# Pooling pass of a four-layer graph network: the sum of gathered rows and turned features made by TensorE in PSUM instead of by VectorE

## The reference, cut to what matters

```python
m = node_feats[src] + edge_feats
mx = jax.ops.segment_max(m, dst, num_segments=n)
ex = jnp.exp(m - mx[dst])
denom = jax.ops.segment_sum(ex, dst, num_segments=n)
a = ex / denom[dst]
agg = jax.ops.segment_sum(m * a, dst, num_segments=n)
h = jax.nn.relu(agg @ mlp_w.T + mlp_b)
return h * scale + node_feats
```

## Time and profile before

| | |
|---|---|
| median of three runs | 4112.33 us |
| lowest and highest | 4110.33 and 4114.03 us |
| the profiled execution, its time | 4113.25 us |
| its span in the trace | 4111.4 us |
| first gather of the pooling pass starts at | 3531.25 us |
| last gather of the pooling pass starts at | 4026.06 us |
| last addition of the pass (line 1356) starts at | 4051.14 us |
| share of the span busy: PE, DVE, ACT, POOL | 57%, 53%, 44%, 64% |

### The profile page before, as it was taken

One profiled execution on the slowest core, in us unless ns is written; L12 is line 12 of the kernel. 1 busy time (PEld: TensorE's weight loads), 2 busy tenths in 40 slices (PEclk: granted clock), 3 DMA queues, 4 the chain that ended last, 5 costly groups with the idle time before them and its releaser, 6 DMA issues.

```text
span 4111.4 us, 44915 instructions
## 1 busy us (share of the span) xinstructions
PE 2340.2 (57%) x10010; PEld 1838.4 (45%) x10010; DVE 2173.5 (53%) x5063; ACT 1822.6 (44%) x4227; POOL 2646.8 (64%) x2793
## 2 busy tenths in 40 slices
PE   6777775344442445444555565655655555467765
PEld 4665653343442434342333353434544344356654
DVE  5888873455564555555222223333434444666667
ACT  2887864343432434335434344343254432344543
POOL 4777712777753777744777727777467776477771
PEclk9999997555555555555555578778855555688887
DMA  6555522343422334323555533333267877455551
GB/s 190 151 161 154 161 59 48 78 86 80 84 60 55 81 78 84 77 49 100 156 160 157 159 87 105 105 105 105 62 191 202 217 212 195 124 155 155 158 155 38
DMA packets 589252, 497.67 MB, mean 121 GB/s; under 512 B 73835, under 2 KB 530592, under 8 KB 588656
## 3 DMA queue, kind: packets, MB, share of 16 engines
q0 software_dynamic: 101696, 235.14, 22.8%
q1 hardware_dynamic: 484630, 254.57, 22.3%
q10 hardware_dynamic: 2684, 5.18, 0.4%
HBM read 426.04 MB, written 68.57 MB: 120 GB/s over the span
## 4 chain that ended last, share of the span: by engine, by line
POOL 50%; issue 19%; PE 12%; DVE 12%; DMA 4%; DVEq 1%; ACT 1%; POOLq 0%; SPq 0%; ACTq 0%
POOL big L595 24%; POOL big L608 18%; POOL y_and_h L622 9%; PE ps L741 5%; DVE y_and_h L1384 3%; DMA big<-table_sage,src_block 2%; DVE ps L1376 2%; DVE big L1356 2%; PE ps L664 2%; PE ps L891 1%; PE ps L678 1%; PE ps L888 1%; DVEq L416 1%; DMA big<-table_gat,src_idx 1%; DVEq L1376 1%
## 5 line engine op out<-in xcount | busy, mean ns | idle before, releaser
L595 POOL DMA_INDIRECT big<-table_sage,src_block x1173 | 1109.9, 946 | 559.9 <-issue 346.3
L608 POOL DMA_INDIRECT big<-table_gat,src_idx x832 | 787.6, 947 | 484.7 <-issue 247.6
L1356 DVE TENSOR_TENSOR big<-big,ps 128x257 f32 (+3 forms) x1664 | 591.9, 356 | 220.5 <-issue 15.5
L622 POOL DMA_INDIRECT y_and_h<-table_pool,src_block x391 | 376.9, 964 | 169.0 <-issue 118.9
L595 POOL DMA_INDIRECT big<-table_mlp,src_block x391 | 371.7, 951 | 166.0 <-issue 117.4
L1144 ACT ACTIVATE rows<-iota,dst_rel 128x128 f32<-128x128 f32 x768 | 243.7, 388 | 260.2 <-PE ps L891 169.9
L1356 DVE TENSOR_TENSOR y_and_h<-y_and_h,ps 128x256 f32 x416 | 175.0, 421 | 340.0 <-PE ps L888 294.4
L1166 ACT ACTIVATE y_and_h<-y_and_h 128x128 f32<-128x128 f32 (+1 forms) x26 | 8.0, 309 | 676.6 <-DVE y_and_h L1593 676.6
L741 PE MATMUL ps<-w_sb,ea_sb 128*128 128x256 f32 x832 | 210.8, 397 | 127.2 <-DVE y_and_h L1384 116.6
L1770 DVE TENSOR_TENSOR_SCAN big<-ps,big 128x512 f32<-128x512 f32 x98 | 125.4, 1280 | 286.5 <-PE ps L917 286.5
L995 PE MATMUL ps<-big,y_and_h 128*128 x624 | 197.8, 472 | 115.7 <-DVE big L1869 114.5
(11 more groups left out here) (299 smaller groups left out, 5631.5 us busy)
## 6 DMA issues: line engine op xcount, KB each, us to landing
big<-in_ea_blocks SPq DMA_DIRECT2D x194, 256.0 KB, 4.0
ea_sb<-in_ea_blocks SPq DMA_DIRECT2D x416, 64.0 KB
ea_sb<-rel_rows SPq DMA_DIRECT2D x208, 128.0 KB
prefix_blocks<-big SPq DMA_DIRECT2D x97, 256.0 KB, 2.4
big<-prefix_blocks SPq DMA_DIRECT2D x97, 256.0 KB, 4.0
below_blocks<-big SPq DMA_DIRECT2D x97, 256.0 KB, 2.7
rows<-in_ea_rows SPq DMA_DIRECT2D x97, 256.0 KB
big<-table_sage,src_block POOLq DMA_INDIRECT x1173, 2.8
```

The costliest lines, as they stand in the source:

```text
L595: pool.indirect_dma_start(ring[:, (block + RING_FIRST[k]) % (n * G), :], None, table[k], bass.IndirectOffsetOnAxis(src_block[:, block:bloc ...
L608: pool.indirect_dma_start(ring[:, step % GAT_RING, :], None, table[k], bass.IndirectOffsetOnAxis(src_idx[:, step:step + 1], 0))\
L622: pool.indirect_dma_start(pool_rows[q][:, i, :], None, table["pool"], bass.IndirectOffsetOnAxis(src_block[:, block:block + 1], 0)).then_in ...
L1356: dve.tensor_tensor(to, to, bank_of(j), ALU.add).then_inc(accumulated, 1)
```

## The change

`turn_below` becomes `make_edge_terms`: PE waits for the gathered rows too, and behind each product that turns a block of features it does a second one, with the identity as the stationary operand and the gathered rows as the moving one, which accumulates into the same place in PSUM. The addition on DVE in line 1861 goes, and with it the semaphore `below_turned`; `edge_terms_ready`, for which ACT, POOL and SyncE wait, is now raised by PE.

```diff
@@ SyncE
-                        sp.wait_ge(below_turned, j - POOL_LOADS + 1)
+                        sp.wait_ge(edge_terms_ready, j - POOL_LOADS + 1)
@@ TensorE
-            def turn_below(j):
+            def make_edge_terms(j):
                 q = j % POOL_LOADS
                 pe.wait_ge(below_loaded[q], 16 * (j // POOL_LOADS + 1))
                 if j >= POOL_LOADS:
                     pe.wait_ge(exp_ready, j - POOL_LOADS + 1)
+                pe.wait_ge(pool_gathered[j % POOL_GATHER], 16 * sum(size_of(i) for i in range(j % POOL_GATHER, j + 1, POOL_GATHER)))
                 for i in range(size_of(j)):
-                    mm = pe.matmul(bank_groups(q)[:, i, :], pool_below[q][:, i, :], ident[:, :], start=True, stop=True)
-                mm.then_inc(below_turned, 1)
+                    pe.matmul(bank_groups(q)[:, i, :], pool_below[q][:, i, :], ident[:, :], start=True, stop=False)
+                    mm = pe.matmul(bank_groups(q)[:, i, :], ident[:, :], pool_rows[j % POOL_GATHER][:, i, :], start=False, stop=True)
+                mm.then_inc(edge_terms_ready, 1)
@@ VectorE, join_edges
-                rows_of, bank = pool_rows[j % POOL_GATHER][:, 0:n, :], bank_groups(q)[:, 0:n, :]
+                rows_of = pool_rows[j % POOL_GATHER][:, 0:n, :]
                 dve.wait_ge(pool_gathered[j % POOL_GATHER], gathers)
-                dve.wait_ge(below_turned, j + 1)
-                dve.tensor_tensor(bank, bank, rows_of, ALU.add).then_inc(edge_terms_ready, 1)
                 dve.wait_ge(pool_ea_loaded[q], 16 * (j // POOL_LOADS + 1))
                 dve.tensor_tensor(pool_ea[q][:, 0:n, :], pool_ea[q][:, 0:n, :], rows_of, ALU.add).then_inc(values_ready, 1)
```

More of the change, by code:

```diff
@@ L371, in program @@
         below_loaded = [sem(f"below_loaded{q}") for q in range(POOL_LOADS)]
-        below_turned, edge_terms_ready, values_ready = sem("below_turned"), sem("edge_terms_ready"), sem("values_ready")
+        edge_terms_ready, values_ready = sem("edge_terms_ready"), sem("values_ready")
         exp_ready, edges_scaled = sem("exp_ready"), sem("edges_scaled")
@@ L1001, in _ @@
                 if q < NBG:
-                    turn_below(q)
+                    make_edge_terms(q)
                 if q >= 2:
```

## The result

The changed kernel takes 4120.3 us, median of 20 executions (4114.74 to 4125.15), beside 4112.52 for the kernel before in 20 of its own. The ratio is 1.0015, with a 95% interval of 1.0009 to 1.0021. The prediction was 4111, a gain of 1.6 us; the kernel became 7.8 us slower. That lies just inside the 8.2 us that I took as no change, yet the interval excludes a ratio of one, and the profile shows the place.

The account below looks back on a forecast made before the run. POOL's issue of gathers was taken as the bound; -6.6 us at the scaling and +5.0 for delayed gathers gave -1.6 on the median 4112.33, so 4111 us. Four fifths lay between 4104 and 4124.

Parts of the forecast that it names:

- What bounds the pass: POOL issues gathers as fast as it can, about 1.25 us apart, and the other engines follow.
- Line 1861 gives nothing by itself: Removing DVE's addition at the landing, 0.70 us a round, 68 us in all, only lengthens DVE's next wait.
- PE's second product and wait, nothing: Eight more matmuls a round on PE, behind the gather: no cost, at most 4 us at clock 0.83.
- Rival 2: PE becomes the bound because its clock stays or falls: 4134 at 0.80, 4166 at 0.75; chance 0.05.
- The end of the pass, nothing: After the last landing, PE's six further matmuls and DVE's spared 0.56 us change nothing, within 0.5 us.
- The hold: A gather starting inside a DVE addition with two SBUF inputs ends 0.82 us past that addition's end.
- SyncE's loads wait for the scaling just as before. All of this: nothing.: In each round, PE's later terms delay nobody, and SyncE's loads still wait for DVE's scaling; no cost.
- The landing intervals of before taken for those of after: Old times from fourth gather's end to DVE's release, median 1.59 us, were kept, giving 8 delayed rounds.
- Hits neither cure nor feed themselves: A gather delayed by line 1863 leaves the next round's phase unchanged, so delays neither stop nor cause others.
- The scaling comes clear, -6.6 us: DVE's line 1869 would start 0.12 us after a gather and delay none: the present 6.6 us loss goes.
- +5.0 for hits: Line 1863, now released by the landing, delays gathers in 8 rounds at 0.63 us each: 5.0 us lost.
- Rival 1: Line 1863 lands on the gather in most rounds: 4137 for half of the rounds, 4167 for all; chance 0.16.

Follow-up runs that it names:

- placeholder run: The changed kernel with an addition of the old kind (PSUM and SBUF in), result unused, put back on DVE; 4109.94 us beside 4109.33, ratio 1.0002.
- placed kernel: The changed kernel with SyncE's loads held back and DVE's order register load, wait, addition, line 1863, addition, scaling, two additions; 4107.97 us beside 4112.92, ratio 0.9987.

## Why the prediction was wrong, step by step

- **What bounds the pass**: right. POOL issues with 0.30 us between gathers in 385 of 391 cases, and the pass is as long as its gathers are.
- **Line 1861 gives nothing by itself**: right. DVE's wait at the landing is 182.4 us in place of 120.9.
- **PE's second product and wait, nothing**: right. The clock was granted at 0.97 with the denser work, which was the assumption, and the placeholder run measures 1.0002. Rival 2 did not come.
- **The end of the pass, nothing**: right, within 0.1 us. The last addition at the landing and the sums behind the last scaling stand 6.29 apart, against 6.28 in the earlier trace rows:

```profile
4037.91 0.56 DVE L1863 TENSOR_TENSOR rows<-rows,y_and_h 128x384 f32<-128x384 f32 x1 [0.65 <-DMA y_and_h<-table_pool,src_block]
...
4044.20 4.11 PE L997 MATMUL ps<-big,y_and_h 128*128 x16 [0.86 <-DVE big L1869]
```

- **The hold**: right, in its rule (0.82 us past the end of the DVE instruction: 3706.59 + 0.69 + 0.82 = 3708.10 = 3706.73 + 1.37) and in its price, 0.63 a hit: a lone hit, at the landing of round 93, held one gather to 1.45 and one to 1.07, 0.63 in sum. The border that it put at 0.02 to 0.05 us lies at 0.043 to 0.047. The Trainium skill's sentence on the shared interface (GPSIMD Engine Reference, Specifications), taken for every overlap, would have given 4167. The two SBUF inputs are in its words, and the traces agree; what they add is that an overlap costs POOL nothing unless the gather's start lies inside: the placed kernel's line 1863 lies across the end of the gather of 3742.72, which took 0.95 as ever.
- **"SyncE's loads wait for the scaling just as before. All of this: nothing."** This is the step that failed. The wait is the same, but what it waits for moved by 0.6 us against the gathers. In a round without a hold the issue fell from +0.5 us to between -0.08 and +0.01 around the fourth gather's end, and there two landings in three are late.
- **The landing intervals of before taken for those of after**: wrong for that reason. I counted 8 hits from the old distribution; 39 of the 98 new intervals were at 1.9 us or more, where 7 had been.
- **"Hits neither cure nor feed themselves"**: wrong. I followed one hit to the next round's gather and stopped ahead of SyncE. A hit puts the scaling on the fourth gather and the load 0.79 ahead of its end; that gather landed late in 16 rounds of 16, its scaling holds a gather of the round after, and this puts line 1863 ahead of the next. The cycle has two rounds.
- **The scaling comes clear, -6.6 us**: wrong in the changed kernel, where it still held 43 gathers for 6.6 us, because of the late rounds. With the loads held back it is 14 for 2.1 us.

The sum against the profile: forecast +5.0 for hits and -6.6 for the scaling. In the trace, line 1863's holds went from 1.7 to 11.9 us (+10.2) and the scaling's from 5.4 to 6.6 (+1.2): +11.4, and the pass grew by 11.24. Rival 1 named the right instruction and the right gather, at 0.63 a hit in half of the rounds; it came in 42, a good part of them lighter than a full hit, and for a cause that it did not name.

**What stays open**: why load packets among a gather's packets make it land 0.4 to 0.9 us later. The order in time is shown in all eight traces, and moving the issue away removes most of the late landings. In late rounds the median packet of the fourth gather starts as ever (0.85 us behind its end against 0.82 in the other rounds of the changed kernel), while the last one ends at 1.83 instead of 1.22. What holds these last ones back is not visible, nor what makes the few rounds late that have no load packet near.

## What to carry to other kernels

When an instruction off the critical path goes, follow everything behind it on its queue to the DMAs that its end releases, and place those on the bound engine's timeline too: here 0.6 us of DVE slack, given away for nothing, moved two loads onto a gather's end, and the pass grew by 11 us. Where a phase between two engines matters, don't carry an interval's old distribution over a change that shifts its neighbours; ask whether a hit shifts the phase of the next round, by at least two rounds. Where DVE and POOL's gathers share a pass, put DVE's instructions with two SBUF inputs between gather starts and those that read PSUM across them; that, with loads held back, beat both kernels (0.9987), though by 5 us only.

## What the runs showed of the hardware

- A gather's landing depends on what SyncE issues around its end. In the changed kernel it came 1.5 to 1.8 us behind that end with the load at +0.3 to +0.6 us, 1.85 to 2.4 in 20 rounds of 28 at -0.08 to +0.01 us, and 2.3 to 2.5 in all 16 rounds at -0.8. The load's first packet runs 1.0 to 1.1 us behind its issue.
- A gather that starts 0.047 us or more behind a DVE instruction with two SBUF inputs, and over about 0.13 us ahead of its end, ends 0.81 to 0.83 us behind it. One that starts at most 0.043 us behind it takes 0.94 to 0.95 us as ever, and DVE's instruction takes 0.72 to 0.77 in place of 0.68.
- A register load of 0.34 us on DVE behind the wait for a gather put the first addition 2.15 us behind the gather's end in the round shown; ahead of the wait, in the placed kernel's round, it came at 1.77.
- The same kernel takes about 4113 us in some groups of runs and 5037 to 5058 in others, and one chip number had both. In the latter PE stops for 0.3 to 1.9 us between products of one group with no wait in the trace.
